# Row stage of a convolution, attention and expert kernel: the third normalising moved from VectorE to ScalarE

## What is computed

```python
def _block(x, ...):
    y = _dcn(x, ...)                                   # ends in  y @ w_out + b_out
    x = x + gamma1 * _ln(y, ln1_g, ln1_b)
    m = _gelu(x @ w_fc1 + b_fc1) @ w_fc2 + b_fc2
    x = x + gamma2 * _ln(m, ln2_g, ln2_b)
    return x
...
def _ln_t(v, eps=1e-05):
    m = jnp.mean(v, axis=-1, keepdims=True)
    s = jnp.var(v, axis=-1, keepdims=True)
    return (v - m) / jnp.sqrt(s + eps)
...
t = _to_tokens(x)
t = t + _L1_attn_ref(_ln_t(t), ...)
t = t + _L1_ffn_ref(_ln_t(t), ...)
```

## Time and profile before

| | |
|---|---|
| median of 3 runs | 3811.91 us (3811.78 to 3816.86) |
| the profiled execution | 3811.91 us, span 3809.8 us |
| PE busy over the span | 3185.4 us, 84% |
| VectorE busy | 2923.3 us, 77% |
| ScalarE busy | 1584.8 us, 42% |
| GpSimd busy | 839.4 us, 22% |
| the row stage | from 1931 us to 2184 us of the span |

### The profile page before, as it was taken

How to read it: one execution, slowest core, us unless ns; L and a number is a source line. 1 busy time by engine, 2 the same in 40 slices (tenths; PEclk the granted TensorE clock), 3 DMA queues, 4 the chain that set the end, 5 groups by cost and what they waited for, 6 DMA issues and landing times. The chain is left out here.

```text
span 3809.8 us, 40876 instructions
## 1 busy us (share of the span) xinstructions
PE 3185.4 (84%) x11501; PEld 1833.3 (48%) x11501; DVE 2923.3 (77%) x4733; ACT 1584.8 (42%) x3465; POOL 839.4 (22%) x856
## 2 busy tenths in 40 slices
PE   5999169999999999999966469999999999430797
PEld 3555135555555555555544234454454554420575
DVE  4888489999999999999959757777677674530476
ACT  1444163333343333344035366647557453110464
POOL 1455100000000000000049701121121121237255
PEclk9999689999999999999988689999999999555898
DMA  3576532121222121121045210010010000301331
GB/s 84 120 187 165 107 46 31 27 27 27 32 32 30 27 27 27 27 29 25 0 111 203 71 38 1 1 31 21 1 51 1 17 18 0 96 14 40 110 97 50
DMA packets 193545, 195.05 MB, mean 51 GB/s; under 512 B 68815, under 2 KB 164439, under 8 KB 192960
## 3 DMA queue, kind: packets, MB, share of 16 engines
q1 hardware_dynamic: 184608, 185.74, 21.6%
q0 software_dynamic: 8800, 7.70, 0.6%
HBM read 96.11 MB, written 110.92 MB: 54 GB/s over the span
## 5 line engine op out<-in xcount | busy, mean ns | idle before, releaser
L781 PE MATMUL deform_acc<-deform_prod,all_ident 128*128 128x392 f32 x4096 | 1379.4, 495 | 76.0 <-DVE deform_prod L866 70.4
L781 PEld LDWEIGHTS deform_acc<-deform_prod,all_ident 128*128 128x128 f32 x4096 | 769.5, 190 | 681.4 <-DVE deform_prod L866 177.9
L866 DVE TENSOR_TENSOR deform_prod<-deform_xw,deform_wd 128x1568 f32<-128x1568 f32 x512 | 908.6, 1786 | 19.4 <-DVE deform_wd L826 11.3
L1584 PE MATMUL attn_ps_r<-attn_prob,attn_xs 128*128 128x448 f32 (+1 forms) x1400 | 599.1, 559 | 28.9 <-POOL attn_xs L1486 28.9
L1680 ACT ACTIVATE attn_prob<-attn_ps_e,attn_nm 128x448 f32<-128x448 f32 (+1 forms) x700 | 438.1, 631 | 363.4 <-DVE attn_nm L1767 360.6
L1767 DVE TENSOR_REDUCE attn_nm<-attn_ps_e 128x1 f32<-128x448 f32 (+1 forms) x700 | 407.2, 614 | 34.6 <-PE attn_ps_e L1572 32.9
L745 ACT ACTIVATE deform_wd<-deform_zeros 128x3136 f32<-128x3136 f32 x32 | 90.1, 2815 | 808.4 <-DVE deform_prod L866 808.4
L1584 PEld LDWEIGHTS attn_ps_r<-attn_prob,attn_xs 128*128 128x128 f32 (+1 forms) x1400 | 266.3, 195 | 240.0 <-issue 178.8
L1483 POOL TENSOR_TENSOR attn_xs<-attn_xa,attn_wz 128x889 f32<-128x889 f32 (+1 forms) x100 | 166.5, 1690 | 775.9 <-DVE attn_wz L1788 775.9
L1036 POOL MEMSET rows_half<- 128x4 f32 x1 | 0.1, 101 | 1524.7 <-POOLq L67 1524.7
L1798 DVE TENSOR_TENSOR attn_xr<-attn_xr,attn_ps_r 128x448 f32<-128x448 f32 x252 | 155.7, 618 | 155.0 <-PE attn_ps_r L1584 153.9
(11 more groups left out here) (325 smaller groups left out, 4070.3 us busy)
## 6 DMA issues: line engine op xcount, KB each, us to landing
offsets_masks<-offs_om SPq DMA_DIRECT2D x56, 378.0 KB
deform_om<-offsets_masks SPq DMA_DIRECT2D x256, 82.7 KB
deform_xw<-projected SPq DMA_DIRECT2D x256, 73.5 KB
dispatched<-rows_zero SPq DMA_DIRECT2D x1, 16512.0 KB
experts_bi<-dispatched SPq DMA_DIRECT2D x32, 516.0 KB, 5.5
projected<-offs_zero SPq DMA_DIRECT2D x13, 680.0 KB
projected<-offs_zero SPq DMA_DIRECT2D x15, 544.0 KB
projected<-offs_zero SPq DMA_DIRECT2D x27, 272.0 KB
```

Source lines behind the costliest of these rows:

```text
L781: mm = pe.matmul(out, ident[:, :], prod[:, s % NPROD, i, :], start=False, stop=(s == NCHUNK - 1 and i == NXH - 1))
L866: nc.vector.tensor_tensor(prod[:, s % NPROD, :, :].rearrange("p d (y x c) -> p d y x c", y=BY, x=UX), x, spread(w.rearrange("p (d y x) -> ...
L1584: mm = pe.matmul(ps_r[n % 2][:, 0:BK], xs[0:rows, at + i, j, :], prob[0:rows, at + i, j * BK:(j + 1) * BK], start=(i == 0), stop=(i == len ...
```

## The change

The third normalising moves to ScalarE, in the form that the other two have. GpSimd makes `negm` and `shift` for it too. ScalarE's step ends with four ACTIVATEs per batch, from `y_all` into `x_all`, that signal `xc_ok`. As buffers are reused every second batch, GpSimd waits before its third group for the normalising two batches back, and VectorE waits before its third aggregation for the shift two batches back.

```diff
-        negm = t.sb("negm", [LANES, 2, 2, QR])
-        shift = t.sb("shift", [LANES, 2, 2, QR])
+        negm = t.sb("negm", [LANES, 2, 3, QR])
+        shift = t.sb("shift", [LANES, 2, 3, QR])
...
                         pool.wait_ge(agg[s], m + 1)
+                        if s == 2 and m >= 2:
+                            pool.wait_ge(xc_ok, m - 1)
                         pool.tensor_scalar(ve[:, q, s, 0:w], mv[:, q, s, 0:w, 1], EPS, None, ALU.add).then_inc(eps[s], 1)
-                        if s < 2:
-                            pool.tensor_scalar(negm[:, q, s, 0:w], mv[:, q, s, 0:w, 0], -1.0, None, ALU.mult)\
-                                .then_inc(neg[s], 1)
+                        pool.tensor_scalar(negm[:, q, s, 0:w], mv[:, q, s, 0:w, 0], -1.0, None, ALU.mult).then_inc(neg[s], 1)
                         pool.wait_ge(eps[s], m + 1)
                         pool.tensor_tensor(rs[:, q, s, 0:w], ve[:, q, s, 0:w], half[:, 0:w], ALU.pow).then_inc(rstd[s], 1)
-                        if s < 2:
-                            pool.wait_ge(rstd[s], m + 1)
-                            pool.wait_ge(neg[s], m + 1)
-                            pool.tensor_tensor(shift[:, q, s, 0:w], negm[:, q, s, 0:w], rs[:, q, s, 0:w], ALU.mult)\
-                                .then_inc(shift_ok[s], 1)
+                        pool.wait_ge(rstd[s], m + 1)
+                        pool.wait_ge(neg[s], m + 1)
+                        pool.tensor_tensor(shift[:, q, s, 0:w], negm[:, q, s, 0:w], rs[:, q, s, 0:w], ALU.mult)\
+                            .then_inc(shift_ok[s], 1)
...
                     normalise(n, 1, LAG1, ps_m, tok_ok)
+                    if there(n, LAG2 + 1):
+                        m, q, w = batch(n, LAG2 + 1)
+                        act.wait_ge(shift_ok[2], m + 1)
+                        for j in range(w):
+                            last = nc.scalar.activation(x_all[:, m * QR + j, :], y_all[:, m * QR + j, :], ACT.Identity,
+                                                        bias=shift[:, q, 2, j:j + 1], scale=rs[:, q, 2, j:j + 1])
+                        last.then_inc(xc_ok, 1)
...
                         dve.wait_ge(stat[s], m + 1)
+                        if s == 2 and m >= 2:
+                            dve.wait_ge(shift_ok[2], m - 1)
...
                     aggregate(n, 2, LAG2)
-                    if there(n, LAG2 + 1):
-                        m, p, w = batch(n, LAG2 + 1)
-                        dve.wait_ge(rstd[2], m + 1)
-                        for j in range(w):
-                            last = nc.vector.tensor_scalar(x_all[:, m * QR + j, :], y_all[:, m * QR + j, :],
-                                                           mv[:, p, 2, j, 0:1], rs[:, p, 2, j:j + 1],
-                                                           ALU.subtract, ALU.mult)
-                        last.then_inc(xc_ok, 1)
```

## The result

| | before | after |
|---|---|---|
| median | 3815.87 us (7 runs, 3811.78 to 3820.00) | 3828.34 us (7 runs, 3823.27 to 3833.82) |
| the profiled execution | 3811.91 us, span 3809.8 | 3833.82 us, span 3832.0 |
| VectorE busy over the span | 2923.3 us | 2877.3 us |
| ScalarE busy | 1584.8 us | 1623.6 us |
| GpSimd busy | 839.4 us | 850.6 us |

What follows compares the result with a forecast made beforehand. GpSimd's list, walked without a stop, was taken to bound the row stage; 21 steps x 0.82 = 17.2 us plus 2.0 at the end gave +19.2 on 3811.9, so 3831 us (main case, chance 0.55), range 3813 to 3843.

Steps and rivals of the forecast that it cites:

- GpSimd sets the pace, VectorE's relief is worth nothing: Row stage: GpSimd walks its list without waits, so removing VectorE's 98 L1236 instructions gains nothing directly.
- +0.45 us on GpSimd's undelayed list: GpSimd's third group: added negation and product lengthen it from 1.32 to 1.77 us, the undelayed step to 8.03.
- The on-time step, 9.39 us: Step with ScalarE on time: 8.03 plus hits on second negation 0.47, third shift 0.41, next L1045 0.48 us.
- The late step, about 9.5 us: Step with ScalarE's first normalising at 3.0 us, not 1.85: delays 0.6 (second power), 0.5 (second shift), 0.4 (next L1045).
- 21 steps at the full price: GpSimd's third groups up to batch 20: 21 steps at +0.82 us each, 17.2 us.
- ScalarE's new work, 1.50 us for four: Four added SBUF-to-SBUF ACTIVATEs a batch on ScalarE: 1.50 us, taken from the PSUM form, bounds 1.1 and 2.4.
- The end, three stores behind batch 20: Stage end: batch 20's normalising sets it, three store groups left; it follows ScalarE's second normalising, +2.0 us.
- The signs: Signs of being right: L1064 9.3 to 9.6 us apart, GpSimd without waits, VectorE idle about 2 us a step.
- VectorE as the bound: Rival, row stage: with L1236 gone GpSimd's delays go too, step 8.03, -11 us, 3801; chance 0.10.
- Longer shut-outs by the power: Rival, GpSimd's second power: it holds VectorE's L1216, which then delays the shift, 0.5 us a step, 3841; chance 0.10.
- Fewer collisions: Rival, GpSimd's step: being shut out costs the same 1.07 us as before, step 9.10, +11 us, 3823; chance 0.20.
- ScalarE as the bound: Rival, ScalarE's loop over two steps: ends first if new work exceeds 3.1 us; at 3.9, step 9.8, 3838; chance 0.05.

Runs made afterwards that it cites:

- GpSimd's additions alone: Kernel before, with GpSimd also making the third negation and shift, which nobody reads; VectorE keeps the third normalising: stage 268.6 us, ratio 1.0047.
- the other order: Kernel after, with the third shift on VectorE and ScalarE's new normalising between its first and second: stage 249.2 us, ratio 1.0000.
- the two runs that don't have it there: GpSimd's additions alone, stage 268.6 us; and kernel after with ScalarE's new normalising between its first and second, stage 267.5 us.
- the shift on VectorE: Kernel after, with the third shift made by one VectorE instruction instead of on GpSimd: stage 259.1 us, ratio 1.0012.

## Why the prediction was right, and where it was off

- **GpSimd sets the pace, VectorE's relief is worth nothing.** Held for this change. VectorE lost 44 us of 150 and the step grew; with GpSimd's additions alone the stage grew by 16.1 us. With the relief and without the additions it grew by 6.6 us in ScalarE's order of the change, and shrank by 3.3 only in the other order. So the additions suffice for the loss, but the two costs do not add up: taking away the additions gives back 7.6 of 14.2 us, because the place of ScalarE's work is the next bound.
- **+0.45 us on GpSimd's undelayed list.** Held: a third group that is not hit takes 1.77 us from its first start to that of L1071 (2011.89 to 2013.66), as forecast, where it was 1.32.
- **The on-time step, 9.39 us.** Measured 9.41 for the step shown, with the collisions at the three places named. Four of the 17 steps are of this kind, and all of those in the run with GpSimd's additions alone that take 9.41 to 9.43.
- **The late step, about 9.5 us.** Its length held where ScalarE is as late as was laid out, 1.2 us: six steps of 9.43 to 9.47 us. Two things in it did not. The second power is not held by an L1204 that begins inside it; the shift behind it and the third L1047 are (0.62 and 0.77 us in the step shown). And there are steps between on time and late, which the prediction did not lay out: with ScalarE 0.2 to 0.7 us late, five of six took 8.84 to 8.98 us. In the one shown, the power of 2075.11 has its usual 1.04 us although L1212 begins in it, at 2075.61, and is still running when it ends. Elsewhere powers were held, in the kernel before this one for 1.70 us:

```profile
2084.23 1.70 POOL L1050 TENSOR_TENSOR rows_rs<-rows_ve,rows_half 128x4 f32<-128x4 f32 x1
...
2084.36 0.68 DVE L1204 TENSOR_TENSOR rows_z<-rows_z,rows_gg 128x512 f32<-128x512 f32 x1
```

Here L1204 came 0.13 us behind the power's start, and the power ended 0.89 us after L1204 did. At 2067.15, with L1204 0.12 us behind, it took 1.09 us. So at 0.12 to 0.13 us the kernel before shows both outcomes. In the kernel after, the powers that took 1.44 to 1.59 us are those where L1212 or L1224 began with them or up to 0.16 us before them, and from 0.07 us behind the power's start on each kept its 1.03 or 1.04 us. That a power reads its input early and needs nothing afterwards would fit; no run shows it. Because of the short steps the mean came to +0.62 us, not +0.82: 17 steps gave 10.5 us, not 13.9.
- **21 steps at the full price.** The price was 0.82 us; it came to 0.62 in the 17 steps, and that is what the sum had too large. Parts of the stage, us:

| from, to | before | after | GpSimd's additions alone |
|---|---|---|---|
| start to the fourth `x2b`, same work | 47.58 | 46.37 | 49.03 |
| the next two steps | 17.17 | 18.80 | 18.88 |
| 17 steps | 147.11 | 157.63 | 159.15 |
| the last of the 18 `x2b` to attention | 40.65 | 43.91 | 41.53 |

The two steps before the 17, the first with a third group, cost +1.6 us, as forecast (2 x 0.82). The last part, two steps and the tail, cost +3.3 where 3.6 was forecast (up to the store of batch 20 it is 19.92 us against 16.68). With 10.5 for the 17 steps this is +15.4 us, where 19.2 was forecast. The first part, where the work is the same, was 1.2 us shorter, which no term foresaw and the change does not explain; it brings the stage to +14.2. The measured median, +12.5, lies near it.
- **ScalarE's new work, 1.50 us for four.** Measured 1.65. Within the bounds, and off the path: ScalarE still waits some 0.8 to 2.1 us before its second normalising.
- **The end, three stores behind batch 20.** Held; the 24 us behind it did not change. The +2.0 for batch 20 behind ScalarE's second normalising is borne out by the two runs that don't have it there: their last part is 41.5 us, 2.4 less than in the kernel after.
- **The signs.** VectorE's waiting is 2.8 us a step rather than about 2. GpSimd's waiting for aggregates was named as a sign of being wrong; it occurs once in 150 us, for 0.6.
- **The rivals.** VectorE as the bound: refuted: with VectorE relieved the step grew, and with GpSimd's additions alone it grew as much. Longer shut-outs by the power: no, VectorE ran beside it in both kernels. Fewer collisions: what happened in five of 17 steps is a mild form of it, and the result lies between it (3823) and the main case (3831); the interval of the total, 9.5 to 18.3 us, takes in its +11, and the main case's +19.2 lies just outside. ScalarE as the bound: not in the steps of this kernel, but it was the next behind GpSimd, as the alternating steps with the shift on VectorE show, and earlier than I had reckoned, in a kernel with a shorter list.
- **The rule on the shared pair.** The Trainium skill, SBUF — State Buffer, "Who interferes with whom", has a VectorE instruction with two SBUF inputs contend with a GpSimd instruction that reads SBUF. That half is what the collisions shown here bear out. That the first to issue keeps the pair for the whole instruction, which the same page of the Trainium skill says of this pairing in "SBUF: two separate sides", fits VectorE's 0.69 us and GpSimd's 512-element sum, and does not fit the power.

Open: what in a small GpSimd instruction is shut out. The rows point at its beginning, but no run varied the size. Open too is why VectorE and ScalarE fall into one kind of step or another.

## What to carry to other kernels

Where two engines both look full, find the one whose list runs without waits; relieving the other was worth at most 3.3 us here, and a few small instructions added to the first cost at least their full length on every step, here 16 us for 50 instructions of 0.2 us, of which the undelayed list accounts for some 11 (25 x 0.45). Count for such an engine, beside its own list, the places where its partner's two-input instructions meet it: a hit instruction of 0.2 us took 0.5 to 0.8 us here, and all hits together 1.1 to 1.8 us of a step of 8.0 to 9.3. A move of work is worth its while if it takes the pace-setter's list down, as moving one large sum did, and one then has to look for the next chain and for the new places to collide.

## What was not expected of the hardware

- In these rows two-input instructions of VectorE on 128 x 512 that begin before a small instruction of GpSimd hold it up for as long as they run: 0.73 us for 0.23 (2083.87), 0.62 for 0.20 (2087.59). But a power that began 0.50 us ahead of such an instruction (2075.11) kept its 1.04 us.
- The third normalising took 1.65 us for four on ScalarE from SBUF to SBUF, the first and second 1.50 from PSUM.
- A later start of one engine can shorten a step: 8.94 us with VectorE 0.73 us later, 9.41 with it on time. At 1.2 us later nothing is left of it, 9.43 us.
